# Lattice attention: the sine-gauss product goes to VectorE, rounding and all row scaling to GpSimd

## The reference, cut to what matters

```python
scores = einsum(q, k) / sqrt(64)
scores = scores * where(int(abs(scores)*1618) % 9 in (0, 3, 6), 1/PHI, 1.0)
attn = softmax(scores)
attn = attn * (sin(C1*attn) * exp(-attn*attn/PHI) + cos(C2*attn))
ctx = attn @ v ;  out = ctx @ Wo + bo
```

## Time and profile before

| | us |
|---|---|
| median of 3 runs | 5878.8 |
| the profiled execution, its own time | 5868.64 |
| its span | 5866.9 |
| TensorE matmul busy | 4792.8 (82%) |
| VectorE busy | 4141.1 (71%) |
| ScalarE busy | 3988.8 (68%) |
| GpSimd busy | 3773.1 (64%) |

### The profile page before, as it was taken

The page is one execution under the profiler, slowest core; times in us unless marked ns, Lnnn a source line. Parts: engine busy times, 40 slices in busy tenths (PEclk is TensorE's granted clock), DMA queues, the critical chain, the costliest instruction groups (busy, mean ns, idle before and its releaser), DMA issues. The chain is left out here.

```text
span 5866.9 us, 98280 instructions
## 1 busy us (share of the span) xinstructions
PE 4792.8 (82%) x27646; PEld 2698.8 (46%) x27689; DVE 4141.1 (71%) x7553; ACT 3988.8 (68%) x5466; POOL 3773.1 (64%) x3599
## 2 busy tenths in 40 slices
PE   2688888888888888888888888888888869997899
PEld 1344444444444444444444444444444436554566
DVE  2577777777777777777777777777777656665664
ACT  1577777777777777777777777777777734444332
POOL 4577777777777777777777777777777634443233
PEclk9799999999999999999999999999999879999999
DMA  0000000000000000000000000000000000000000
GB/s 5 23 9 8 8 8 8 8 9 8 10 8 8 8 8 8 8 8 8 9 8 10 8 8 8 8 8 8 8 9 8 4 9 1 2 2 15 3 6 7
DMA packets 34184, 45.24 MB, mean 8 GB/s; under 512 B 24521, under 2 KB 24585, under 8 KB 34058
## 3 DMA queue, kind: packets, MB, share of 16 engines
q1 hardware_dynamic: 32010, 43.49, 2.8%
q0 software_dynamic: 2048, 0.14, 0.1%
HBM read 39.40 MB, written 4.19 MB: 7 GB/s over the span
## 5 line engine op out<-in xcount | busy, mean ns | idle before, releaser
L588 PE MATMUL banks<-ident,att 128*128 128x128 f32 x8192 | 1148.2, 287 | 410.0 <-DVE ag L520 252.1
L588 PEld LDWEIGHTS banks<-ident,att 128*128 128x128 f32 x8192 | 944.6, 147 | 1004.1 <-DVE ag L520 616.9
L630 PE MATMUL banks<-kT,qT 128*128 128x512 f32 x2048 | 1144.8, 658 | 278.9 <-DVE mx L549 269.6
L390 POOL TENSOR_TENSOR sinb<-sinb,ag 128x1024 f32<-128x1024 f32 x512 | 1281.5, 2506 | 85.4 <-ACT sinb L461 70.4
L540 DVE SCALAR_TENSOR_TENSOR mag<-near,mag 128x512 f32<-128x512 int32 x1024 | 857.7, 842 | 483.6 <-POOL near L406 474.2
L400 POOL TENSOR_SCALAR mag<-mag 128x512 f32<-128x512 f32 x1024 | 689.5, 678 | 573.1 <-DVE mag L540 539.0
L647 PE MATMUL outp<-sinb,vo 128*64 128x512 f32 x2048 | 1046.3, 636 | 0.0
L647 PE MATMUL outp<-work,vo 128*64 128x512 f32 x2048 | 1046.3, 636 | 0.0
L406 POOL TENSOR_SCALAR near<-mag 128x512 int32<-128x512 f32 x1024 | 794.0, 775 | 363.9 <-ACT mag L479 300.3
L479 ACT ACTIVATE mag<-banks 128x512 f32<-128x512 f32 x1024 | 599.2, 592 | 283.1 <-PE banks L630 283.0
L497 DVE TENSOR_TENSOR work<-banks,work 128x1024 f32<-128x1024 f32 x512 | 625.1, 1221 | 192.8 <-ACT work L455 189.8
(11 more groups left out here) (198 smaller groups left out, 6357.7 us busy)
## 6 DMA issues: line engine op xcount, KB each, us to landing
x<-xT_dram SPq DMA_DIRECT2D x128, 256.0 KB, 3.5
xT_dram<-xT SPq DMA_DIRECT2D x8, 256.0 KB, 2.9
out<-hres SPq DMA_DIRECT2D x8, 256.0 KB, 2.6
base<-in_L_tok_turns,idx POOLq DMA_INDIRECT x64, 2.3
wqk<-in_L_attn_Wq SPq DMA_DIRECT2D x64, 16.0 KB
wqk<-in_L_attn_Wk SPq DMA_DIRECT2D x64, 16.0 KB
wqk<-in_L_attn_bq SPq DMA_DIRECT2D x64, 0.2 KB
wqk<-in_L_attn_bk SPq DMA_DIRECT2D x64, 0.2 KB
```

The lines of the kernel that those rows point to most:

```text
L390: nc.gpsimd.tensor_tensor(sinb[:, k % RING], sinb[:, k % RING], ag[:, k], ALU.mult).then_inc(tmul, 1)
L588: mm = nc.tensor.matmul(turn_pair(k)[:, c, i * P:(i + 1) * P], att[:, p, 4 * half + i, kt * P:(kt + 1) * P], ident[:], is_transpose=True, ...
L630: nc.tensor.matmul(score_bank(n), qT[:, p, (n // 2) * P:(n // 2 + 1) * P], kT[:, p, (n % 2) * 512:(n % 2 + 1) * 512], start=True, stop=Tru ...
```

## The change

The sine x gauss product moves from GpSimd's queue to VectorE's, at the same step and behind the gauss term. GpSimd now normalises all eight row tiles and does the rounding to whole turns, six steps after the exponential and not three. The semaphore `weights2` goes.

```diff
-        NORM, TURNS = 1, 3
-        DVE_ROWS = (TB // 2 - 1, TB - 1)
+        NORM, TURNS = 1, 6
 # GpSimd
-                        if a - P3 in SINE:
-                            k = SINE.index(a - P3)
-                            wait(pool, sined, TB * g + k + 1)
-                            wait(pool, agd, TB * (g + 1))
-                            nc.gpsimd.tensor_tensor(sinb[:, k % RING], sinb[:, k % RING], ag[:, k],
-                                                    ALU.mult).then_inc(tmul, 1)
-                        if a - NORM in EXP and EXP.index(a - NORM) not in DVE_ROWS:
+                        if a - TURNS in EXP:
+                            j = EXP.index(a - TURNS)
+                            wait(pool, nned, TB * g)
+                            held(pool, weights, TB * g + j + 1)
+                            nc.gpsimd.tensor_scalar(nturn[:, j], att[:, p, j], ROUND, -ROUND,
+                                                    ALU.add, ALU.add).then_inc(turned, 1)
+                        if a - NORM in EXP:
 # VectorE
-                        if a - NORM in EXP and EXP.index(a - NORM) in DVE_ROWS:
-                            j = EXP.index(a - NORM)
-                            wait(dve, recip, TB * g + j + 1)
-                            nc.vector.tensor_scalar(att[:, p, j], att[:, p, j], rs[:, j:j + 1], TURN,
-                                                    ALU.mult, ALU.mult).then_inc(weights2, 1)
-                        if a - TURNS in EXP:
-                            j = EXP.index(a - TURNS)
-                            if j in DVE_ROWS:
-                                wait(dve, weights2, 2 * g + j // 4 + 1)
-                            else:
-                                wait(dve, weights, (TB - 2) * g + j + 1 - j // 4)
-                            wait(dve, nned, TB * g)
-                            nc.vector.tensor_scalar(nturn[:, j], att[:, p, j], ROUND, -ROUND,
-                                                    ALU.add, ALU.add).then_inc(turned, 1)
+                        if a - P3 in SINE:
+                            k = SINE.index(a - P3)
+                            wait(dve, sined, TB * g + k + 1)
+                            wait(dve, agd, TB * (g + 1))
+                            nc.vector.tensor_tensor(sinb[:, k % RING], sinb[:, k % RING], ag[:, k],
+                                                    ALU.mult).then_inc(tmul, 1)
 # TensorE, fill
-                wait(pe, weights, (TB - 2) * g + (TB // 2 - 1) * (half + 1))
-                wait(pe, weights2, 2 * g + half + 1)
+                wait(pe, weights, TB * g + TB // 2 * (half + 1))
```

More of the change, by code:

```diff
@@ L273, in lattice @@
         names = ("consts loadq loadv projd qk_sb vald v_sb qk mags rounded kept factor filtered bias expd "
-                 "recip weights weights2 turned xpose squared gauss agd cosd acd nned sined tmul av evac folded "
+                 "recip weights turned xpose squared gauss agd cosd acd nned sined tmul av evac folded "
                  "outd").split()
         (consts, loadq, loadv, projd, qk_sb, vald, v_sb, qk, mags, rounded, kept, factor, filtered, bias,
-         expd, recip, weights, weights2, turned, xpose, squared, gauss, agd, cosd, acd, nned, sined, tmul,
+         expd, recip, weights, turned, xpose, squared, gauss, agd, cosd, acd, nned, sined, tmul,
          av, evac, folded, outd) = (sem("l_" + n) for n in names)
```

## The result

The changed kernel takes 7208.53 us (median of 6 runs, 7203.84 to 7216.89) beside 5871.39 us of the kernel before: a ratio of 1.2302, 95% interval 1.2279 to 1.2324. It is 23% slower, 1337 us more, or 20.9 us for each of the 64 heads. I had forecast 5785 us and a range of 5630 to 5950; the result lies far outside.

The account below looks back on a forecast made before the run. Bound by waits between in-order queues, no engine full. Turnover -3.7, gauss stage +2.3, sine stage 0 gave -1.4 us a head, x 64 = -90 us: 5779 from 5868.64, forecast as 5785 us, range 5630 to 5950.

Parts of the forecast that it names:

- the price of a rounding on GpSimd: Eight roundings per head moved to GpSimd, taken at 1.12 us each, bounds 1.1 and 1.6.
- the slower rival: GpSimd's queue between first fill and near 9 bounds the gauss stage: 5930 us, chance 0.24.
- The gauss stage: First fill to first cosine product, 29.80 us before: forecast +2.3 us a head, bounds -1 to +6.5.
- The queue sum: GpSimd's queue from first fill to near 9: 24.2 us of instructions plus 2 for keeps, 26 against 23.3 before.
- caught up behind: Gauss stage: part of the 3 us added before near 9 is regained later, where GpSimd has little, leaving +2.3.
- The turnover: Last cosine product to next head's first fill, 16.22 us before: forecast -3.7 us a head, bounds -1 to -5.
- The sine stage: First to last cosine product, 23.87 us before: forecast 0 us a head, bounds -1 and +3.
- The bound of 2.4 us: High bound for each moved product on VectorE, from an instruction that ran behind a GpSimd product; 1.2 was taken.
- The row scalings of VectorE: Two per head moved to GpSimd: VectorE loses 2.3 us busy time, GpSimd gains two scalings.
- the sum for e3: Forecast before e3: turnover -3.7 us, gauss stage about 0, sine stage 0; 5635 us, say 5600 to 5700.
- a rounding above 1.3 us: Sign named beforehand that the forecast is wrong: GpSimd's roundings take longer than 1.3 us.
- a gauss stage above 33.5: Sign named beforehand that the forecast is wrong: first fill to first cosine product exceeds 33.5 us.

Follow-up runs that it names:

- e6: Changed kernel with a cheap multiply-by-1, add-constant instruction in the rounding's place on GpSimd, turns left out of the computation: 6056.16 us, ratio 1.0341.
- e9: As e6, but the cheap instruction is issued fourteen steps after the exponential instead of six: 5840.45 us, ratio 0.9916.
- e3: Changed kernel with the rounding back on VectorE, three steps after the exponential, all eight row scalings on GpSimd: 5876.63 us, ratio 1.0039.
- e4: Kernel before with only the sine x gauss product moved to VectorE; rounding and rows 3 and 7 stay on VectorE: 5749.08 us, ratio 0.9814.

## Why the prediction was wrong

- What failed is the price of a rounding on GpSimd: "the low bound is 1.1; the high bound 1.6 ... I take 1.12, since the arithmetic is alike". It measured 3.86 us in place and 3.63 alone, and the arithmetic is what is not alike: all TENSOR_SCALAR rows of GpSimd in the lattice before pair a multiplication with a multiplication or an addition, and none adds twice. This term alone is 1138 of the 1337 us (e6). The same wrong price is in the slower rival, which named the right place (GpSimd's queue from the first fill on) and put it at 5930. My high bound was the longest row of another operation, so it bounded that operation's contention and not the unseen one's cost.
- The gauss stage: +2.3 forecast, +24.0 measured (+24.6 in the mean). Near my price it was +3.5 and +5.7 in two heads, +5.2 in the mean (e6): even there the forecast was too small. The queue sum added up GpSimd's busy time and part of the holds, and let part be "caught up behind"; it took GpSimd's queue as running through and had no term for the waits back and forth. In e6 VectorE waits 12.4 us a head for near (6.8 before), and GpSimd in turn 13.4 for VectorE's keep (549.7/41; 8.3 before, 357.0/43). e9, which only moves the cheap instructions, gives 4.1% back.
- The turnover: -3.7 forecast, -2.65 measured (-2.8 in the mean); right in kind. The reciprocal comes 7.2 us after the last cosine product, where I had 6.4 and before it was 9.5. On the way VectorE waits 0.51, 0.51 and 0.65 us for near and factor (its timeline after):

```profile
2138.36 1.22 DVE L496 TENSOR_TENSOR work<-banks,work 128x1024 f32<-128x1024 f32 x1
...
2141.28 0.69 DVE L531 SCALAR_TENSOR_TENSOR mag<-near,mag 128x512 f32<-128x512 int32 x1 [0.51 <-POOL near L405]
2141.89 1.22 DVE L525 TENSOR_TENSOR sinb<-sinb,ag 128x1024 f32<-128x1024 f32 x1
2143.62 0.69 DVE L531 SCALAR_TENSOR_TENSOR mag<-near,mag 128x512 f32<-128x512 int32 x1 [0.51 <-POOL near L405]
2144.97 0.69 DVE L540 CUSTOM_DVE_ANT_0 att<-mag,banks 128x512 f32<-128x512 f32 x1 [0.65 <-POOL mag L399]
...
2145.58 0.16 DVE L513 RECIPROCAL rs<-ssum 128x1 f32<-128x1 f32 x1
```

- The sine stage: 0 forecast, -0.1 measured (-0.4 in the mean), as forecast. The product on VectorE takes 1.232 us in the mean (I had 1.2), 96% of the stage is VectorE's, and TensorE at 22.9 us is as full. The bound of 2.4 us, behind a GpSimd instruction, did not come about: GpSimd is busy for 7.5 us there.
- The row scalings of VectorE that I moved for the price of their busy time cost 2.3% with the rounding on VectorE (e3 against e4). In the prediction they stood only as busy time on GpSimd, and in the sum for e3 not at all. What they cost in the changed kernel itself no run separates.
- Two signs that I had named showed it at once: a rounding above 1.3 us, and a gauss stage above 33.5.
- Two slips in the arithmetic changed little: six roundings and a scaling are 6.1 us and not 5.8 (6 x 0.825 + 1.157), and 5779 plus the 10 us of the median is 5789 and not 5785.

## What to carry to other kernels

The price of an operation that an engine has not yet run is not the price of its neighbour in the trace with the same shape and type: the pair of arithmetic operations alone made 1.05 or 3.63 us here. Where a forecast hangs on such a price, the rows of other operations give no high bound for it, and one run that times the forms alone settles it. And when work moves to an engine with idle time, look at which short hand-offs are queued behind it there: the same eight cheap instructions cost 4.1% more when issued eight steps earlier.

## What the runs showed of the hardware

- GpSimd, one input, 128x1024 float32, nothing beside it: mult/mult, mult/add and add/mult 1.05 us; add/add, add/subtract, subtract/subtract and mult/subtract 3.63 us; one addition alone 2.77 us (three with their gaps 8.49, below). Writing bf16 in place of float32 changes neither add/add nor mult/add, and add/mult into int32 takes 1.04. The size of the constants changes nothing for add/add. A column operand in add/add adds 0.08.

```profile
57.97 8.49 POOL L1519 TENSOR_SCALAR b_f<-b_src 128x1024 f32<-128x1024 f32 x3
```

- So a second operation, multiply by one, makes an addition on GpSimd faster: 1.05 against 2.77 us.
- TensorE's granted clock was 0.71 in the mean over the gauss stage of the changed kernel, where its matmuls were busy for 30 of 54 us, and 1.00 in the two other stages of the same head. After 8 us without a matmul it stood at 0.50 from 2072 to 2078 us, and a fill took 1.97 us instead of 1.04.
